# The transposes of head 1 in the first attention, moved from behind the next scores to behind head 0 of their own round

## What is computed

```python
scores = jnp.einsum('bhqd,bhkd->bhqk', wq, wk) * scale
mask = jnp.triu(jnp.ones((ws, end), dtype=bool), k=1)
scores = jnp.where(mask[None, None], neg, scores)
attn = jax.nn.softmax(scores, axis=-1)
outs.append(jnp.einsum('bhqk,bhkd->bhqd', attn, wv))
```

## Time and profile before

| | |
|---|---|
| median of three runs | 2684.61 us |
| the profiled execution | 2688.99 us, of which the span in the trace is 2687.0 us |
| TensorE busy | 2390.7 us (89%) |
| VectorE busy | 1575.9 us (59%) |
| ScalarE busy | 1234.0 us (46%) |
| granted TensorE clock, mean | 0.978 of full |
| maxima of the first attention, L1067 | 512 instructions, 483 ns each |
| exponentials, L779 | 512 activations, 542 ns each |
| transposes of the probabilities, L473 | 1280, 277 ns each |

### The profile page before, as it was taken

The page is one execution under the profiler, slowest core; times in us unless marked ns, Lnnn a source line. Parts: engine busy times, 40 slices in busy tenths (PEclk is TensorE's granted clock), DMA queues, the critical chain, the costliest instruction groups (busy, mean ns, idle before and its releaser), DMA issues.

```text
span 2687.0 us, 37065 instructions
## 1 busy us (share of the span) xinstructions
PE 2390.7 (89%) x13032; PEld 1320.1 (49%) x13032; DVE 1575.9 (59%) x3089; ACT 1234.0 (46%) x2842; POOL 696.5 (26%) x1001
## 2 busy tenths in 40 slices
PE   8889999988888999898888999998888899998776
PEld 3655444445465544354546554454555655444343
DVE  4664624468676561557867555065786746525687
ACT  5753211268584412128858331213876823121485
POOL 0002321037301232013720213102570021310265
PEclk9999999999999999999999999989999999999988
DMA  8001100010300200000030101101003010100000
GB/s 291 17 10 64 33 16 32 0 48 9 110 16 10 70 28 21 27 16 32 9 124 2 57 23 28 39 9 48 1 16 116 2 56 23 44 0 1 1 1 32
DMA packets 58988, 99.43 MB, mean 37 GB/s; under 512 B 13364, under 2 KB 13748, under 8 KB 58296
## 3 DMA queue, kind: packets, MB, share of 16 engines
q1 hardware_dynamic: 58808, 97.06, 10.8%
HBM read 88.66 MB, written 8.39 MB: 36 GB/s over the span
## 4 chain that ended last, share of the span: by engine, by line
PE 63%; ACT 15%; DVE 11%; issue 7%; POOL 3%; DMA 0%; ACTq 0%; DVEq 0%; POOLq 0%; SPq 0%
PE psum L379 21%; PE psum L373 17%; ACT prob L779 6%; PE psum L457 3%; PE psum L523 2%; PE psum L473 2%; ACT xT L808 2%; POOL f_y L362 2%; ACT f_a L966 2%; PE psum L760 1%; DVE f_top L1356 1%; PE psum L665 1%; PE psum L543 1%; PE psum L732 1%; PE psum L594 1%
## 5 line engine op out<-in xcount | busy, mean ns | idle before, releaser
L373 PE MATMUL psum<-xT,weights 128*128 128x512 f32 x1152 | 508.5, 596 | 19.1 <-DMA weights<-in_a_k 10.4
L373 PEld LDWEIGHTS psum<-xT,weights 128*128 128x128 f32 x1152 | 215.1, 191 | 271.5 <-issue 253.2
L379 PE MATMUL psum<-weights,mixed 128*128 128x512 f32 x768 | 337.3, 595 | 3.1 <-DVE mixed L1302 3.1
L1067 DVE TENSOR_REDUCE neg_max<-psum 128x1 f32<-128x128 f32 (+3 forms) x512 | 217.6, 483 | 136.6 <-PE psum L466 71.2
L379 PE MATMUL psum<-weights,xT 128*128 128x512 f32 x640 | 288.9, 596 | 2.4 <-DVE recip L1259 1.6
L1394 POOL TENSOR_SCALAR var<-stats 128x1 f32<-128x1 f32 x192 | 61.7, 321 | 796.3 <-DVE stats L1012 796.3
L779 ACT ACTIVATE prob<-psum,neg_max 128x128 f32<-128x128 f32 (+3 forms) x512 | 263.1, 542 | 4.5 <-DVE neg_max L1067 4.4
L1407 POOL TENSOR_TENSOR f_a<-f_a,f_z 128x256 f32<-128x256 f32 x256 | 193.0, 759 | 166.9 <-DVE f_a L1074 163.9
L379 PEld LDWEIGHTS psum<-weights,mixed 128*128 128x128 f32 x768 | 143.4, 190 | 179.9 <-issue 173.3
L1042 DVE TENSOR_TENSOR x<-psum,x 128x512 f32<-128x512 f32 x128 | 88.4, 690 | 223.4 <-PE psum L379 161.4
L1074 DVE SCALAR_TENSOR_TENSOR f_a<-f_g,conv_w,f_a 128x256 f32<-128x256 f32 x256 | 173.1, 676 | 52.3 <-ACT f_a L966 51.6
(11 more groups left out here) (242 smaller groups left out, 4063.3 us busy)
## 6 DMA issues: line engine op xcount, KB each, us to landing
xT<-in_xT SPq DMA_DIRECT2D x8, 1024.0 KB, 6.6
x<-in_x SPq DMA_DIRECT2D x8, 1024.0 KB, 8.3
out<-x SPq DMA_DIRECT2D x16, 512.0 KB, 2.8
weights<-in_a_k SPq DMA_DIRECT2D x4, 1024.0 KB, 5.0
weights<-in_a_q SPq DMA_DIRECT2D x4, 1024.0 KB, 5.0
weights<-in_a_v SPq DMA_DIRECT2D x4, 1024.0 KB, 5.3
w1f<-in_w SPq DMA_DIRECT2D x4, 1024.0 KB, 14.8
w2f<-in_w SPq DMA_DIRECT2D x4, 1024.0 KB, 17.4
```

The source lines that it names most:

```text
L373: last = mm(bank[:, 0:n], weights[weight][:, c, heads(g)], rhs(c), start=(c == 0), stop=(c == C - 1))
L379: last = mm(bank, lhsT(c), weights[weight][:, c, :], start=(c == 0), stop=(stop and c == C - 1))
L1067: last = v.tensor_reduce(sb["neg_max"][:, n, qc, j:j + 1], bank[:, o:o + P * (qc + 1)], AX.X, ALU.max, negate=True)
```

## The change

In `schedule`, the step that transposes head 1 of group i moves from behind the scores of round i+1 to behind the transposes of head 0 in round i. ScalarE's copy of it is made at that step instead of ahead of the exponentials of the next round.

```diff
         if 1 <= i <= len(GROUPS):
-            steps += [("a_turn", i - 1, 1), ("a_turn", i - 1, 2)]
+            steps.append(("a_turn", i - 1, 2))
...
         if i < len(GROUPS):
-            steps.append(("a_turn", i, 0))
+            steps += [("a_turn", i, 0), ("a_turn", i, 1)]
...
                 elif kind == "a_score":
                     i, = arg
-                    if i > 0:
-                        copy_turned(i - 1, 1)
                     exponentials(i, range(G) if i == 0 else range(1))
                 elif kind == "a_turn":
                     i, j = arg
-                    if j == 0 or (j == 1 and i == len(GROUPS) - 1):
+                    if j < 2:
                         copy_turned(i, j)
```

## The result

The changed kernel takes 2709.05 us (median of four runs, 2706.23 to 2711.84) where the kernel before, on the same chip, took 2684.97. The ratio is 1.0089, with a 95% interval of 1.0077 to 1.0101. It is slower by 24.1 us; 24.3 were predicted.

What follows compares the result with a forecast made beforehand. Bound before by the round of scores, mask, transposes and exponentials; after, by a loop through VectorE's copy of head 3. Periods +6.18, head +0.2, tail -0.3: 6.1 us a batch, 24.3 in all, 2709 us, range 2697 to 2721.

Steps and rivals of the forecast that it cites:

- The gain of the exponentials: Each round: with head 1 copied during the scores, exponentials start 0.44 us (two tiles) or 0.34 us (512 columns) earlier.
- The new wait and the loop through VectorE: Head 1 waits for VectorE's copy of head 3 to free their bank; next scores 0.36 or 0.45 us later per round.
- The handing over of 0.15 us: From the end of VectorE's copy of head 3 to head 1's transposes: 0.15 us, between nothing and 0.3.
- the 0.56 for the transposes: From the start of head 1's four transposes to the next scores: 0.56 us, between 0.52 and 0.63.
- "about 1 us" of the signs: Expected in the changed timeline: head 1's transposes wait for VectorE's copy some 17 times a batch, about 1 us each.
- The period of two tiles: Start to start of scores in rounds of two tiles, 11 a batch: 6.05 us, where it was 5.69.
- The period of 512 columns: Start to start of scores in rounds of 512 columns, 6 a batch: 5.93 us, where it was 5.48.
- reciprocals' copy 752.04 - 751.13 = 0.91 later: Rounds of 512 columns: reciprocals' copy 0.91 us after the first exponential, at s + 3.06, s being the start of the scores.
- Head and tail of a batch: Outside the 17 periods: +0.2 us before the scores of group 2, -0.3 us after those of group 19.
- The clock: Rival: TensorE's longer idle drops the clock to 1.2 GHz in the rounds, 105 us over 68 periods, about 2814 us; 4%.
- The sum: Periods, head and tail together: 6.1 us a batch, 24.3 us for four batches, giving 2709 us; 88%.
- free in time: Rival: head 1's bank is free in time, exponentials set periods of 5.25 and 5.14 us, 28 us faster, 2657 us; 5%.

Runs made afterwards that it cites:

- the two edits of VectorE's work: On the changed kernel: maxima of head 3 taken twice, 2777.62 us; head 3 copied ahead of its maxima, 2687.09 us. On the kernel before: 2684.86 and 2696.02 us.
- the bank: Changed kernel with four score banks and bank 7 for head 1 alone: 2730.83 us; control, kernel before with four score banks: 2783.42 us.

## Why the prediction was right, point by point

- *The gain of the exponentials.* Predicted 0.44 and 0.34 us earlier; measured 2.70 to 2.27 (0.43), and 2.49 to 2.15 (0.34). Right.
- *The new wait and the loop through VectorE.* Right, and shown by the two edits of VectorE's work, by the exchange of heads 0 and 1, and by the bank. The handing over of 0.15 us, seen once a batch before, is 0.14 where it now happens each round (775.74 to 775.88), and the 0.56 for the transposes is 0.57. The wait itself is shorter than the "about 1 us" of the signs, 0.5 to 0.63.
- *The period of two tiles.* Predicted 6.05, measured 6.04 to 6.05 in all 44 rounds.
- *The period of 512 columns.* Predicted 5.93, measured 5.72 or 5.73 (one of 24 took 5.95). The step that failed is "reciprocals' copy 752.04 - 751.13 = 0.91 later". That distance held a wait: the transposes of the reciprocals had themselves waited for the copy of head 1, and ended just before the copy started. With that copy early the distance is 0.68, and what ends the chain is VectorE, free at s + 4.34. 0.2 us too much in 24 rounds is 4.8 us.
- *Head and tail of a batch.* Predicted +0.2 and -0.3; measured -0.1 and +0.1 in batch 2. At the head, round 0 is 0.43 us longer and round 1 0.52 shorter, where 0.56 and 0.33 were put. With the same early reciprocals the tail should have gained 0.6, as it does in the kernels with the groups of two tiles moved (11.99 and 12.08 instead of 12.63 us). The fall of the clock took that back.
- *The clock.* I had it as a rival that holds for all rounds, 105 us, or not at all. In the rounds it stayed at 1.00. TensorE's idle ahead of head 1 is also shorter than I had put it, 0.63 us, as another 0.5 lies ahead of head 0. In the profiled execution the clock fell once a batch, behind the rounds, after TensorE had been busy for 2.37 of 4.00 us; the longest wait there, 1.69 us for the spread reciprocals, stands there before too, without a fall. Why it falls in one and not in the other is not shown. It costs 0.76 us in the products and 0.85 in the projection (in batch 0 all of it ahead of the projection), 1.6 us a batch, 6 us in all. This is one execution, with a mean clock of 0.974; the other three, at 0.976 to 0.981, have no trace. The Trainium skill (TensorE: Matmul & The Clock Gate, section "A second HAM failure mode: psum-queue depth-cycling") has the clock swing where TensorE idles briefly between groups of matmuls. The trace agrees for the kernel with the maxima taken twice (mean clock 0.964, 1.30 us of idle ahead of head 1), and not for the rounds of the changed kernel (1.00, 0.63 us). The length of one idle piece does not decide it alone: with heads 0 and 1 exchanged it is 1.76 us in a round of two tiles, and 62 of 68 rounds kept 1.00.
- *The sum.* 24.3 against 24.1 us. Two errors of 5 to 6 us cancel in the profiled execution, the rounds of 512 columns and the clock, and that the sums agree so closely is luck; without it, 2704 or 2715 us would still lie inside the range. The rival "free in time" asked for VectorE 0.8 us earlier. With its copy 0.6 us earlier, 22 of the 24 us came back; the full 0.8 was not tried.

## What to carry to other kernels

Before work is moved ahead on the engine that waits, look up who last used the buffer that it claims: a step that fits in idle time is free only if its buffer is free too, and everything behind it in the queue pays for the wait. When a move turns out slower, take the releaser named in brackets on the moved step and ask whether that engine can do this piece first; here a reorder of two instructions on VectorE, with the move and the reorder limited to the groups and rounds of two tiles, made a loss of 24 us into a gain of 18.5. And do not carry a distance between two rows over to a new order before checking whether it holds a wait that the change removes.

## What the runs showed of the hardware that was not expected

The granted clock stayed at 1.00 through the rounds of the changed kernel, 101 us in a batch, with 0.5 to 0.63 us of idle on TensorE ahead of head 1 in each. It fell in over a third of the rounds when VectorE had 0.60 to 0.66 us more to do in each (mean of the execution 0.964, rounds of up to 7.8 instead of 6.7 us), and in 6 of 68 with heads 0 and 1 exchanged. What tips it was not isolated. A loop on another engine can thus cost more than its own length: the same 0.6 us of VectorE's work cost 0 us in one order, and 69 us in the other, of which 43 to 44 are the loop.
